# A gated cross-attention and mixture-of-experts kernel on one core: expert weights fetched a slot earlier, clears in 44 slots, ScalarE's late reads moved

## What is computed

```python
x = x + tanh(g_xattn[0]) * xattn(ctx_1024, layernorm(x), ...)
x = x + tanh(g_ffn[0]) * ffn(layernorm(x), ...)

# xattn: keys and values from 64 context rows and the 64 rows of x itself, 8 heads of 128
xn, ln = layernorm(ctx) * g + b, layernorm(x_n) * g + b
q = ln @ Wq + bq
k, v = split(concat([xn, ln], axis=1) @ Wkv + bkv)
out = softmax(q @ k.T * DH ** -0.5) @ v
return merge_heads(out) @ Wo + bo

# ffn: 8 experts, the best 2 of each row
probs = softmax(x @ Wr + br)
top_p, top_i = top_k(probs, 2)
cw = sum(one_hot(top_i, 8) * top_p)
h = relu(x @ W1[e] + b1[e])
y = h @ W2[e] + b2[e]
out = sum over e of cw[e] * y[e]
```

## Time and profile before

| | |
|---|---|
| median of 3 runs | 800.37 us (799.6, 800.37, 803.32) |
| profiled execution | 800.92 us, of which the span from first to last instruction is 799.2 us |
| TensorE busy | 757.6 us |
| VectorE busy | 523.1 us |
| ScalarE busy | 492.8 us |
| GpSimd busy | 428.3 us |
| moved by DMA | 124.10 MB, mean 155 GB/s |

### The profile page before, as it was taken

One profiled execution on the slowest core, in us unless ns is written; L12 is line 12 of the kernel. 1 busy time (PEld: TensorE's weight loads), 2 busy tenths in 40 slices (PEclk: granted clock), 3 DMA queues, 4 the chain that ended last, 5 costly groups with the idle time before them and its releaser, 6 DMA issues.

```text
span 799.2 us, 17227 instructions
## 1 busy us (share of the span) xinstructions
PE 757.6 (95%) x5306; PEld 634.3 (79%) x5306; DVE 523.1 (65%) x1814; ACT 492.8 (62%) x1615; POOL 428.3 (54%) x443
## 2 busy tenths in 40 slices
PE   7999999999899999999999999999999889879995
PEld 7778777777788787888877888878987768778774
DVE  5636677685858566575869687686758566375545
ACT  4676777776766466565767665766656665554331
POOL 2233365646543535434578665686654686444573
PEclk9999999999999999999999999999999999999998
DMA  6836162644776836463214556274731145543132
GB/s 189 247 146 219 60 238 73 231 161 144 246 265 230 298 127 229 165 199 110 57 37 148 190 172 219 66 213 156 238 117 31 47 136 182 179 115 105 53 89 83
DMA packets 122109, 124.10 MB, mean 155 GB/s; under 512 B 14857, under 2 KB 87842, under 8 KB 122018
## 3 DMA queue, kind: packets, MB, share of 16 engines
q1 hardware_dynamic: 113920, 108.16, 40.8%
q0 software_dynamic: 7168, 14.69, 6.5%
q10 hardware_dynamic: 930, 0.15, 0.1%
HBM read 33.52 MB, written 53.28 MB: 109 GB/s over the span
## 4 chain that ended last, share of the span: by engine, by line
PE 73%; DVE 7%; POOL 6%; issue 6%; ACT 4%; DMA 2%; SPq 1%; ACTq 0%; POOLq 0%; DVEq 0%
PE shared L1500 12%; PE batch L1451 11%; PE batch L1438 10%; PE hid_ps L1361 7%; PE xy_ps L1375 6%; PE batch L1446 5%; PE shared L1284 4%; PE shared L1286 3%; PE shared L1285 3%; ACT probs L798 2%; POOL qT L718 2%; PE xy_ps L1338 2%; POOL yg L718 2%; POOL probs L728 1%; PE batch L1428 1%
## 5 line engine op out<-in xcount | busy, mean ns | idle before, releaser
L728 POOL TENSOR_TENSOR probs<-probs,rsums 128x512 f32<-128x512 f32 x128 | 132.9, 1038 | 244.2 <-DVE rsums L1214 243.6
L798 ACT ACTIVATE probs<-batch,neg_max 128x128 f32<-128x128 f32 x512 | 180.4, 373 | 2.1 <-DVE neg_max L1218 2.1
L878 ACT ACTIVATE qT<-shared,tb 128x512 f32<-128x512 f32 x128 | 87.3, 695 | 96.4 <-PE shared L1286 96.3
L1451 PE MATMUL batch<-pT_sb,kvn 128*128 128x512 f32 x256 | 133.8, 604 | 4.7 <-ACT pT_sb L806 4.7
L1438 PE MATMUL batch<-kvT,qT 128*128 128x128 f32 x1024 | 136.4, 276 | 0.8 <-ACT qT L878 0.8
L704 POOL DMA_INDIRECT sorted<-xn,row_of x112 | 114.8, 1025 | 26.8 <-issue 26.8
L1438 PEld LDWEIGHTS batch<-kvT,qT 128*128 128x128 f32 x1024 | 125.3, 193 | 1.2 <-ACT qT L878 1.2
L1500 PE MATMUL shared<-M,oT 128*128 128x128 f32 x1024 | 125.2, 276 | 0.2
L1500 PEld LDWEIGHTS shared<-M,oT 128*128 128x128 f32 x1024 | 119.5, 192 | 1.1 <-issue 1.1
L1214 DVE RECIPROCAL rsums<-sums 128x4 f32<-128x4 f32 x128 | 23.2, 181 | 137.0 <-ACT probs L798 135.6
L798 ACT ACTIVATION_READ_ACCUMULATOR probs<-batch,neg_max 128x1 f32 x512 | 109.9, 215 | 0.0
(11 more groups left out here) (187 smaller groups left out, 1252.2 us busy)
## 6 DMA issues: line engine op xcount, KB each, us to landing
wt<-wall SPq DMA_DIRECT2D x110, 321.0 KB, 3.2
sorted<-yg SPq DMA_DIRECT2D x63, 512.0 KB, 4.5
xt<-sorted SPq DMA_DIRECT2D x133, 64.0 KB
sorted<-y_sb SPq DMA_DIRECT2D x133, 64.0 KB
kv<-in_ctx_dram SPq DMA_DIRECT2D x16, 256.0 KB
kv<-in_x_dram SPq DMA_DIRECT2D x16, 256.0 KB
xres<-in_x_dram SPq DMA_DIRECT2D x32, 128.0 KB, 2.3
out_dram<-x SPq DMA_DIRECT2D x15, 256.0 KB
```

The costliest lines, as they stand in the source:

```text
L728: nc.gpsimd.tensor_tensor(pv, pv, rsums[:, m % 2, :].unsqueeze(2).broadcast_to([P, 4, P]), ALU.mult).then_inc(probs_ready, 1)
L798: last = nc.scalar.activation(probs[:, m % 2, c * P:(c + 1) * P], batch_ps[m % BANKS][:, c * P:(c + 1) * P], ACT.Exp, bias=neg_max[:, m % ...
L878: nc.scalar.activation(qT[:, g % 2, :, number, :], sh[:, :].rearrange("p (b i) -> p b i", b=GB), ACT.Identity, bias=tb[:, number:number + ...
L1451: nc.tensor.matmul(batch_ps[m % BANKS][:, :], kvn[:, m % KVN, :], pT_sb[:, :], start=True, stop=True).then_inc(o_ready, 1)
```

## The change

Three things are moved; the work is the same. SyncE calls `fetch_weights` for the tile of slot `n+2` in place of `n+1`. `CLEARING` goes from 56 to 44, so that the last clear is issued at slot 44 instead of 56. ScalarE's table read is taken out of its `fetch_weights` into `read_experts`, which is called at the end of slot `n` for the tile of slot `n+2`; its copies stay where they were. The router exponentials get a function of their own, `route_exponentials`, called where they stood for slots below `TAIL` and at the end of the slot from `TAIL` on, which concerns group 15 in slot 134 alone.

```diff
-CLEARING = 56
+CLEARING = 44
...
-                if TILE_AT.get(n + 1, N_TILES) < LATE:
-                    fetch_weights(TILE_AT[n + 1])
+                if TILE_AT.get(n + 2, N_TILES) < LATE:
+                    fetch_weights(TILE_AT[n + 2])
                 if n - 2 in TILE_AT:
                     store_tile(TILE_AT[n - 2])
...
                     keep_turned(n - TURN)
-                g = n // GB - 1
-                if n % GB == 6 and 0 <= g < G:
-                    act.wait_ge(route_step, routed(g) + 2)
-                    nc.scalar.activation(prob[:, :, :], shift[:, :, :], ACT.Exp).then_inc(rexp_done, 1)
+                if n < TAIL:
+                    route_exponentials(n)
                 for what in shared_at(n, "a", "act"):
                     read_out(*what)
                 if TILE_AT.get(n + 1, 0) >= LATE:
...
                 for what in shared_at(n, "c", "act"):
                     read_out(*what)
+                if n >= TAIL:
+                    route_exponentials(n)
+                if TILE_AT.get(n + 2, 0) >= LATE:
+                    read_experts(TILE_AT[n + 2])
...
-            def fetch_weights(i):
+            def read_experts(i):
 
                 if i == LATE:
                     act.wait_ge(experts_ready, 1)
...
                     read_table(mybir.EngineType.Activation, 1, experts, i, N_TILES, E - 1)
+
+            def fetch_weights(i):
+
                 wait(act, y_done, i - WB + 1)
```

More of the change, by code:

```diff
@@ L841, in slot, with route_exponentials @@
                     read_out(*what)
+                if n >= TAIL:
+                    route_exponentials(n)
+                if TILE_AT.get(n + 2, 0) >= LATE:
+                    read_experts(TILE_AT[n + 2])
+            def route_exponentials(n):
+                g = n // GB - 1
+                if n % GB == 6 and 0 <= g < G:
+                    act.wait_ge(route_step, routed(g) + 2)
+                    nc.scalar.activation(prob[:, :, :], shift[:, :, :], ACT.Exp).then_inc(rexp_done, 1)
             experts = {}
-            def fetch_weights(i):
+            def read_experts(i):
                 if i == LATE:
```

## The result

The changed kernel takes 790.03 us (median of 4 executions, 788.34 to 790.77) where the kernel before takes 801.85 (4 executions, 799.6 to 805.14): the ratio is 0.9847, with a 95% interval of 0.9805 to 0.9888. The profiled execution took 790.77 us with a span of 789.0.

A forecast was written before the change was run, and what follows sets the result against it. The prediction took TensorE, busy 757.6 of 799.2 us, to bound the kernel. Gains of 6.49 + 1.43 + 1.87 = 9.8 us brought the 800.37 us median to 790.6 us, range 788.0 to 795.5.

The forecast's parts named there:

- Part 1: SyncE's earlier weight fetch: six TensorE stops go, 6.49 us at list starts and 2.30 us at tiles 54 and 55.
- Part 2: Clears in 44 slots: more clears a slot, no TensorE stop there waits for a DMA, so 0 us.
- Part 3, the last `oT`: ScalarE's first late table read ahead of `oT`: takes back 0.87 of 2.30 us, leaving 1.43 us.
- Part 3, tile 60: ScalarE's second late read: the 3.19 us `xtT` stop shrinks, VectorE's ranking is late next, 1.87 us gained.
- Part 4: Last router exponentials at the end of slot 134: gain counted at tile 60, cost 0 to 0.2 us.
- (a): Rival: ScalarE's reads are short, `oT` isn't late, gain 10.7 us, 789.7 us; chance 0.14.
- (b): Rival: the tail gives nothing, only the list starts' 6.5 us are left, 793.9 us; chance 0.12.
- (c): Rival: SyncE's own waits keep weights late at four list starts, some 3.5 us left, 797 us; chance 0.10.
- (d): Rival: denser clears delay kv and xres rows, 15 us lost against 9.8 gained, about 805 us; chance 0.04.

The follow-up runs named there:

- e1: Kernel before with only SyncE's weight fetch moved to the tile of slot n+2: 791.64 us, ratio 0.9868.
- e5: Changed kernel with CLEARING put back to 56: 800.02 us, ratio to the kernel before 0.9846.
- e2: Kernel before with only CLEARING set to 44 in place of 56: 797.82 us, ratio 0.9935.
- e4: Changed kernel with the last router exponentials put back where they stood: 789.47 us, ratio to the kernel before 0.9841.
- first set of runs: The runs e1 to e4, on the same chip as the third set; the kernel before had a median of 802.37 us.
- third set of runs: The runs a1 to a4, on the same chip as the first set; the kernel before had a median of 810.17 us.
- a1: The changed kernel timed again without a further edit: 795.85 us, ratio to the kernel before 0.9837.
- e3: Kernel before with only ScalarE's edits, the moved table reads and last router exponentials: 798.8 us, ratio 0.9952.
- a2: Changed kernel with VectorE's last ranking of experts divided over slots 134 to 136: 794.14 us, ratio to the kernel before 0.9806.
- e9: Changed kernel with the last ranking divided and ScalarE's first late table read ahead of tile 54's xtT: 798.78 us, ratio to the kernel before 0.9848.
- e6: Changed kernel with CLEARING set to 28: 799.13 us, ratio to the kernel before 0.985.
- e8: Changed kernel with VectorE's last ranking of experts divided, the same edit as a2: 797.84 us, ratio to the kernel before 0.9836.
- a3: Changed kernel with the same edits as e9, timed in another set: 794.28 us, ratio to the kernel before 0.9812.
- a4: Changed kernel with a3's edits, and SyncE reading the first rows of tiles 60 to 67 early: 793.65 us, ratio to the kernel before 0.9808.
- second and third set of runs: The runs e5 to e9, on another chip (kernel before 811.99 us), and a1 to a4, on the first set's chip (810.17 us).

## Why the prediction held, step by step

**The number.** The time came out 0.6 us from the forecast, and this is closer than the working: the forecast gain was 9.8 us and the measured one 11.8. The kernel before took 1.5 us more in the runs of the result than in those that the forecast began from (801.85 and 800.37), which hid most of the 2 us. The steps below are judged by rows and not by that time.

**Part 1, 6.49 + 2.30 us: right.** Six stops gone, in the changed kernel and in e1. The reason given holds as well: nothing else was late next at those six places. The landing of weights hidden behind "issue" was read rightly, since an edit to the fetch alone removed all five stops that were put down to it.

**Part 2, 0: right only in the company of part 1.** e5 shows 0 and e2 shows 4.5 us. The sum was made in an order in which part 1 had already taken the idle time, so it came out right, and its reason stands in the one sentence that clears out of the way "can only help weights which by part 1 are early anyway". The share in the stretch from 100 to 160 us was put at 0.63 and is 0.62 with 216 GB/s, against 0.52 and 181 in the earlier trace rows.

```profile
100.00:160.00 60.00, 58.29 (x385) 45.53 (x385) 41.46 (x149) 43.41 (x152) 36.20 (x35) 1.00 0.62 216
```

**Part 3, the last `oT`: 0.87 forecast, 0.85 found.** The length of the read was taken as 2.76 us and was 2.61. The list by source line shows all three; they still differ by a factor of 1.5:

```profile
L534 ACTq TENSOR_LOAD <-table x3: 1706/1862/2608, 684.0 to 707.8; - x3
```

**Part 3, tile 60: 1.87 forecast, 1.95 found.** The stop for `xtT` was forecast at 0.3 and is 0, the one for `hs` at about 1 us and is 1.24; 3.19 - 1.24 = 1.95. (The working has TensorE ready at 708.8 us; by the earlier trace rows it is 713.59 - 3.19 - 1.43 = 708.97, so that the 0.3 should have been 0.1. VectorE decides there, and the sum doesn't change.)

The estimate of 1.6 us for a read, from the page of the Trainium skill that the prediction names ("Runtime: NRT & Kernel Launch", Instruction fetch mechanics), fits two of the three here (1.71 and 1.86), not the one that has `oT` behind it.

**Part 4, 0 to 0.2: right,** by e4. The forecast had VectorE reach the ranking at 709.1 us with `prob` at 709.2. In the trace it comes at 702.40, 1.1 us behind the end of `prob`, because `hs` and `y_sb` of the tile ahead stand between. So the order in which ScalarE does things did not delay it; e4 shows the same.

**The term that was missing: what a stop takes beyond its idle time.** Between the landmark and tile 60's second product 7 stops with 11.98 us went and 2 with 2.09 came: 9.89 us, and the rows moved by 10.92. The three early stops show it well: from the landmark to the next wait for `table` it was 403.50 - 182.01 = 221.49 us and is 398.39 - 182.72 = 215.67. That is 5.82 for 5.29 of idle time, 0.18 us for each stop. The rows at a stop show where it goes. Two groups of TensorE overlap when nothing is waited for. Ahead of tile 0's first product stands this group, in before and in after:

```profile
215.57 1.06 PE L1438 MATMUL batch<-kvT,qT 128*128 128x128 f32 x8
216.27 1.06 PE L1450 MATMUL batch<-kvT,qT 128*128 128x128 f32 x8
```

After, the product begins 0.90 us behind it (217.17), though the group is listed as 1.06 us long; before it is 3.19 us (218.76), which is 2.29 more for 2.13 of idle time. So 0.16 us is overlap lost. The group behind the stop then takes 1.13 us instead of 1.06. The two make 0.23 us; tiles 8 and 12 have the same, 0.7 us for the three. Of this 0.16 us comes back soon behind tile 0: there TensorE begins a group 0.52 us behind a transpose in after (218.76, 219.28), and 0.36 us behind it in before (220.41, 220.77). That leaves the 0.53.

**The measured gain, 11.8 us, against 10.9 in the traces.** Executions differ in their mean granted clock, and their times follow it. Of 16 executions of the kernel before in the first set of runs, one at 0.997 took 798.8 us, and three at 0.988 to 0.990 took 803.7 to 804.36. The changed kernel's four have 0.995 to 0.997. In the third set of runs the median clock was 0.988 for the kernel before and 0.993 for a1, and the gain 14.3 us. So the part of the gain that the rows don't show, about 1 us in the result and more in the third set, goes with the clock; the two traces compared above have one mean clock, 0.995. Read in stretches of 5 us, every trace has at most two falls of the clock ahead of its last 25 us, where the work runs out and each has some:

| trace | stretches with a lowered clock |
|---|---|
| before | 25 to 35 |
| changed kernel | 10 to 20 |
| e1, e3, e4, a2 | none |
| e2 | 705 to 715, behind the stop for `xtT` |
| e5 | 685 to 695, behind a stop of 3.44 us |
| e9 | 685 to 690, behind one of 2.07 us |
| e6 | 25 to 40, 645 to 655 |
| e8, a3 | 10 to 20 |
| a1 | 25 to 35 |
| a4 | 645 to 650 |

The row of before, in the columns given above, shows one:

```profile
30.00:35.00 5.00, 4.97 (x30) 4.77 (x30) 2.56 (x10) 2.63 (x13) 1.77 (x2) 0.69 0.47 130
```

The places are few, each has stops of its own, and at each the clock falls in some executions and not in others. The kernel before had one such place more than the changed one, the 3.2 us for `xtT`: it fell there in one trace (e2) of the three that have that stop (before, e1, e2). That this is the missing microsecond is likely and not shown; it would take many traces of the kernel before.

**Rivals.** (a) would have had no stop for `oT`: it is there, 0.85 us. (b) would have had the tail give nothing: it gave its share. (c) would have left the four list starts: none stayed. (d) would have had new stops behind clears before 216 us: none, even with `CLEARING` 28.

**What stays open.** In the second and third set of runs ScalarE stands still at places of its program for which no row gives a reason, and TensorE with it: in the last dense products in all eight traces, and before `xtT` of tile 55 in six of them (not in a2 and a3). In a1:

```profile
686.05 0.38 ACT L833 ACTIVATE xtT<-xy_ps 128x256 f32<-128x256 f32 x1 [2.80 <-issue]
...
776.17 0.69 ACT L878 ACTIVATE qT<-xy_ps,b_all 128x512 f32<-128x512 f32 x1 [6.71 <-PE shared L1422]
```

```profile
686.57 1.13 PE L1387 MATMUL xy_ps<-wt,hs 128*128 128x128 f32 x8 [1.99 <-issue]
...
777.48 3.54 PE L1440 MATMUL batch<-wall,qT 128*128 128x128 f32 x16 [2.32 <-ACT qT L878]
```

In the first set of runs and in the result neither is there. In a1 TensorE's stops by it are 1.99, 0.47 and 2.32 us, and the product group behind the last takes 3.54 us instead of 1.95, at a lowered clock: 6.4 us, of which 0.56 comes back since the stop for `oT` is 0.29 and not 0.85. From the landmark to the end a1 takes 612.8 us, 6.5 more than the profiled execution of the result, with the same kernel. So this is most of the difference between these two, and the reason that the sets' times aren't set side by side. It isn't the chip alone, since the first and the third set ran on one. Nor does the amount of instructions fetched differ: the profile's two queues of instruction transfers have 43 and 48 packets in both traces. The cause stays open.

## What to carry to other kernels

An idle time of TensorE put down to "issue" can be a DMA: set the issue of the tile's data on its queue, the issue's length and the landing time beside the end of the stop, and if they meet, move the issue forward past what needn't go first. When two edits heal the same stop, try each alone, and don't add their gains; here the gains of e1, e2 and e3 would add up to 10.7 + 4.5 + 3.6 = 18.8 us, where all the edits together give 11.8. When a stop of several microseconds is removed, ask which engine is late next: it took back 1.24 of 3.19 us here, and what stood ahead of `hs` in VectorE's row mattered more than the order of ScalarE's: e4 only divided the stop, e8 took it away. When an experiment is to remove a stop, look first whether the stop is there in the traces it will be compared with; e9, a3 and a4 aimed at 0.85 us where 0.29 stood.

## What the runs showed of the hardware

- A stop of TensorE ahead of these groups costs about 0.2 us beyond its idle time (0.53 us for three, 1.03 us for a net five): 0.16 us of overlap with the group ahead is lost, and the group behind takes 1.13 us instead of 1.06.
- The granted clock fell to half behind a stop of 2.80 us, and behind two of 1.07 and 0.94 us close together, and in other executions with the same stops it didn't (3.19 us in before, 3.27 in e1). The falls cost 2.85 us in e2 and 1.6 in a4.
- A read of up to eight table values into SyncE's registers takes 0.53 to 3.8 us (median 1.68). In the changed kernel it is 0.53 to 3.15 with the same median. On ScalarE the three take 1.63 to 2.76 and 1.71 to 2.61 us.
- With the DMA engines 0.74 busy at 273 GB/s (e6, 60 to 100 us) the work of attention beside it was not delayed: from the stop near 49 us to the landmark it is 133.43 us in e6 and 133.39 in before. Ahead of that, at 0.87 and 307 GB/s, no stop is new, but the clock fell for longer than in before.
